# A second wait in front of each quad of indirect gathers on GpSimd

## What is computed

```python
def _gnn_layer(edge_index, x, edge_attr, norm, We, be, Wn, bn):
    src, dst = (edge_index[0], edge_index[1])
    parts = [x[src], x[dst]]
    if edge_attr is not None:
        parts.append(edge_attr)
    e = jax.nn.relu(jnp.concatenate(parts, axis=-1) @ We + be)
    msg = e * norm[:, None] if norm is not None else e
    agg = jax.ops.segment_sum(msg, dst, num_segments=x.shape[0])
    x_new = jax.nn.relu(jnp.concatenate([x, agg], axis=-1) @ Wn + bn)
    return (x_new, e)
```

## Time and profile before

| what | us |
|---|---|
| median of three runs | 2675.99 |
| lowest and highest of them | 2674.0, 2693.58 |
| the profiled execution | 2685.29 |
| its span, first to last instruction | 2683.2 |
| TensorE busy | 2142.4 (80%) |
| VectorE busy | 1447.8 (54%) |
| GpSimd busy | 1001.1 (37%), of it 824.7 in the 864 gathers of L1512 |
| mean share of TensorE's full clock | 0.875 |

### The profile page before, as it was taken

One profiled execution on the slowest core, in us unless ns is written; L12 is line 12 of the kernel. 1 busy time (PEld: TensorE's weight loads), 2 busy tenths in 40 slices (PEclk: granted clock), 3 DMA queues, 4 the chain that ended last, 5 costly groups with the idle time before them and its releaser, 6 DMA issues. The chain is left out here.

```text
span 2683.2 us, 48362 instructions
## 1 busy us (share of the span) xinstructions
PE 2142.4 (80%) x14264; PEld 1585.6 (59%) x14264; DVE 1447.8 (54%) x4661; ACT 653.0 (24%) x1271; POOL 1001.1 (37%) x1015
## 2 busy tenths in 40 slices
PE   7666679999999657777777678888888677888885
PEld 4222234444444347666666578787877577777774
DVE  6988832332332446656666455555555455555555
ACT  0246731221221122222222322222222211111111
POOL 0765400000000035555555245454553454555550
PEclk8777789999999768878888899999999888889887
DMA  2123550000000343333333255555553333433431
GB/s 81 25 57 83 95 47 1 0 0 0 0 0 0 120 127 107 116 102 114 105 112 108 83 164 160 154 164 165 162 162 117 103 101 97 112 105 106 112 106 38
DMA packets 193650, 242.15 MB, mean 90 GB/s; under 512 B 56276, under 2 KB 120047, under 8 KB 192799
## 3 DMA queue, kind: packets, MB, share of 16 engines
q1 hardware_dynamic: 161023, 172.73, 22.3%
q0 software_dynamic: 31840, 57.21, 9.1%
q10 hardware_dynamic: 576, 9.44, 0.9%
HBM read 149.75 MB, written 69.88 MB: 82 GB/s over the span
## 5 line engine op out<-in xcount | busy, mean ns | idle before, releaser
L1512 POOL DMA_INDIRECT rows<-p_dram,src_i x864 | 824.7, 954 | 751.9 <-PE psum L1623 441.8
L1744 DVE TENSOR_TENSOR agg_t<-psum,agg_t 128x128 f32 x1380 | 394.1, 286 | 466.6 <-remote 263.6
L1603 PE MATMUL psum<-w_c,before 128*128 128x128 f32 x1840 | 440.8, 321 | 24.2 <-issue 23.8
L1592 PE MATMUL psum<-p_sb,pair_src 128*128 x1032 | 257.7, 330 | 151.3 <-issue 85.6
L1677 ACT ACTIVATE rows<-rows 128x512 f32<-128x512 f32 x216 | 136.1, 630 | 901.1 <-DVE rows L1737 608.3
L893 PE MATMUL psum<-adj,parts 128*128 (+2 forms) x1750 | 339.7, 351 | 5.8 <-ACT agg L972 4.4
L1603 PEld LDWEIGHTS psum<-w_c,before 128*128 128x128 f32 x1840 | 305.3, 207 | 27.4 <-issue 27.3
L1728 DVE TENSOR_SCALAR hot_w<-col_f,dst_loc,weight 128x128 f32<-128x128 f32 x864 | 308.5, 360 | 0.5
L1623 PE MATMUL psum<-hot_w,rows 128*128 128x128 f32 x1728 | 279.8, 307 | 29.4 <-issue 27.6
L1592 PEld LDWEIGHTS psum<-p_sb,pair_src 128*128 128x128 f32 x1032 | 188.2, 224 | 175.7 <-issue 173.6
L1599 PE MATMUL psum<-q_parts,hot_all 128*128 x2592 | 270.2, 229 | 15.5 <-issue 15.4
(11 more groups left out here) (241 smaller groups left out, 2590.4 us busy)
## 6 DMA issues: line engine op xcount, KB each, us to landing
e_dram<-after SPq DMA_DIRECT2D x230, 256.0 KB
before<-e_dram SPq DMA_DIRECT2D x230, 256.0 KB
adj<-stage SPq DMA_DIRECT2D x196, 97.8 KB
pair_rows<-sorted_rows SPq DMA_DIRECT2D x129, 128.0 KB
rows<-p_dram,src_i POOLq DMA_INDIRECT x864
hot_all<-dst_rows ACTq DMA_DIRECT2D x2, 3072.0 KB, 15.0
p_dram<-p_sb SPq DMA_DIRECT2D x6, 384.0 KB
records<-record_of,place_i POOLq DMA_INDIRECT x128
```

What stands on the lines that cost most here:

```text
L1512: nc.gpsimd.indirect_dma_start(out=rows[:, b % ROWS, m * D:(m + 1) * D], out_offset=None, in_=p_dram, in_offset=bass.IndirectOffsetOnAxis( ...
L1592: nc.tensor.matmul(o, pair_src[:, i % PAIRS, m, :], t["p_sb"][:, bass.ds(values[m], 1), :], start=True, stop=False)
L1603: mm = nc.tensor.matmul(o, before[:, q % BEFORE, m * P:(m + 1) * P], w_c[:], start=False, stop=True)
L1744: nc.vector.tensor_tensor(a, psum[:, A_BANKS[q % len(A_BANKS)], m * P:(m + 1) * P], a, ALU.add).then_inc(agg_on, 1)
```

## The change

Ahead of the first gather of quad b, from b = 4 on, GpSimd also waits until all four gathers of quad b - 1 have landed. `landed(b)` is the count that `rows_in[b % 4]` has then; it is the same count that `add` waits for on VectorE.

```diff
         def _(pool):
+            def landed(b):
+                earlier = nth * len(range(b % ROWS, REST_QUADS, ROWS))
+                return 16 * QUAD * (earlier + b // ROWS + 1)
+
             def further_rows():
...
                 if b >= ROWS:
+                    pool.wait_ge(rows_in[(b - 1) % ROWS], landed(b - 1))
                     pool.wait_ge(summed, slot_of(b - ROWS) + 1)
```

## The result

The change costs about half a per cent where it was first timed: 2690.37 us median (19 runs, 2675.16 to 2699.26) against 2674.31 us (19 runs) for the kernel before, ratio 1.0048 with the interval 1.0026 to 1.0069. A second comparison gave 2678.40 against 2674.52 us, ratio 1.0028 (1.0004 to 1.0052). Predicted were 2679 us, within 2668 to 2712. The figure fits, but its reason does not: the profile after shows rival B's mechanism in all three passes. The time hardly moved because one pass gained what the two others lost, so the figure is right by luck.

A forecast was written before the change was run, and what follows sets the result against it. TensorE, the busiest engine, was taken to pace the passes and GpSimd's gathers; the added wait would mostly hide in the adds' margin. The median 2676 plus 3 us gave 2679 us, range 2668 to 2712.

The forecast's parts named there:

- rival B: Landing paces the kernel: 0.47 us more a quad in passes one and two, 20 + 27 us, time 2723; chance 0.21.
- slack that hides the wait: Gathers before the adds: rows lie finished 7.7 to 10.2 us, so the wait costs 0 to +15 us; chance 0.74.
- The start behind the landing: GpSimd's next first gather after the last packet: 0.3 us semaphore plus 0.26 us start, together 0.6 us.
- The landing: Time from a quad's last gather to its last packet: about 1.6, 2.0 and 1.3 us in passes one, two, three.
- a small stretch: Landings lengthen on meeting SP's transfers at another time; half of 0.5 us a quad gives 15 to 20 us.
- level with what they needed: GpSimd's idle time a quad in passes one and two: 2.2 and 2.6 us there, 2.2 and 2.6 needed.
- The releasers: What ends waits: landing for well over half of 204 first gathers in passes one and two; TensorE still for VectorE's adds.
- the prediction's own test: Profile after: adds released by the landing of rows would mean the landing paces the kernel.
- Pass three has room: GpSimd's gathers in pass three: 2.5 us idle a quad there, 1.9 needed, so the added wait costs 0 us.
- the replay: Recurrence over all 216 quads by the trace's times: passes one, two, three end 1, 2, 0 us later; +3 taken.
- C: Later gathers put fewer packets beside SP's loads, for which TensorE waits: up to 25 us faster, 2651; chance 0.05.
- GpSimd does not pace anybody: GpSimd in the passes: busy half the time, idle 240 to 259 us a pass before gathers, paced by TensorE's sums.

The follow-up runs named there:

- first pair of profiles: Kernel before and changed kernel, each profiled in the first timing: 2674.31 against 2690.37 us median, ratio 1.0048.
- second pair of profiles: Both kernels, unchanged, profiled once more in a later comparison: before 2674.52 us, changed 2678.40 us, ratio 1.0028.
- the last experiment: Kernel before with the wait for the landing added in pass three alone, timed once more: 2366.14 us against 2228.94, ratio 1.0621.
- The run with quarter transfers: Changed kernel with SP's loads of the layer before and its stores cut to a quarter of their columns: 2577.61 us, ratio 1.1551 to the kernel before.

## Why the prediction was right, and where it was wrong

2679 us lies within 0.5% of what was measured, and that is luck. The mechanism that was given the most weight, slack that hides the wait, did not hold in any pass. The landing paced the gathers, as in B, and passes one and two together lost 20 to 42 us, within what B says; pass three gained as much by something that was in no rival.

**The start behind the landing: right.** 0.3 us for the semaphore and 0.26 us for the start were taken, 0.6 in sum. In the profile after, the median from a quad's last packet to the next first gather is 0.62, 0.65 and 0.60 us. The 0.73 us of rival B belongs to a wait in the sequencer, and exchanging the waits showed it (1.08 us).

**The landing: the term that was mis-sized.** 1.6, 2.0 and 1.3 us were taken, and that is what before has (1.68, 2.07, 1.32). After the change they are 1.91, 2.46 and 1.50 us: 0.2 to 0.5 us more than was taken (0.1 to 0.3 us more than before in the second pair of profiles), where the margin that decided was put at 0.2 us a quad. The text named this way to fail ("if it stretches when its time moves") and gave it 0.21 together with a price of 15 to 20 us for a small stretch. The weights stood the wrong way round. The reading that two of the three passes were level with what they needed was itself the warning: a term of 1.3 to 2.6 us, held fixed, decided it by 0.2.

The rule of the Trainium skill that was weighed ("DMA: Bandwidth & Descriptors", section "Anatomy of one DMA") gave 2.15 us always, by estimate 7.1 us a quad. The medians from one quad's first gather to the next one's are 7.15, 7.45 and 6.61 us in the profile after, so as a price of a gather chain it was near the truth for two passes. The trace agrees with its size and not with "always": landings range from 1.2 us to 5.6 us.

**The releasers: wrong.** First gathers released by the landing in well over half of the cases was right (197 of 204, the number for all three passes), an idle sum "nearly the same" was right by accident (261.1, 302.1, 225.0 for 240, 259, 253 us), and "adds still released by TensorE" was wrong. By the prediction's own test this is B.

**Pass one and two: B's direction, and its size.** B's price for a small stretch was 15 to 20 us, for 0.47 us a quad 20 + 27. Measured: +10.5 and +31.6 us in the first pair of profiles, -5.0 and +25.4 in the second, and +34 us by the experiment with the wait in these two passes alone.

**Pass three: the step that failed.** "Pass three has room", cost 0, held for the sum that stood behind it (1.50 + 0.6 = 2.1 us needed a quad, 2.5 there), and yet 42 of its 72 adds were late. What was wrong is what stands under it, in the replay and in the first paragraph: TensorE's times were carried over as a property of the work. They hold 368 us of pauses that the profile puts down to nothing, and 282 us of those vanish with the added wait. As TensorE got faster, its adds caught up with the landings. So pass three gained 29 to 45 us (the two pairs of profiles, and the experiment with the wait there alone), which no rival had. C (faster, 0.05) had another mechanism, a shorter wait for SP's loads: this wait fell from 12.8 to 6.2 us in pass three, a sixth of the gain.

**"GpSimd does not pace anybody": true of the chips with pauses.** The idle 2.2 to 2.6 us a quad on GpSimd was slack lent by TensorE's pauses. Where these are absent a quad of before takes 5.3 us in pass one (381 us by 72), 5.0 of them GpSimd's own four gathers (4.69 + 0.30), and the chain of landings needs 7.0 (the median of pass three in the last experiment). The run with quarter transfers, the nearest there is to the changed kernel on such a chip, is 349 us over the kernel before. An estimate for the whole change: its passes of the other chip, 1605 us, less 381 + 416 + 382 gives 426 us, a ratio of 1.19. The changed kernel itself was not run on such a chip.

**What stays open.** What the pauses are. The same program has them in three comparisons and hardly any in three others, and where it has them, they are in a stage without these gathers too. What takes them away is open as well: late adds that hold TensorE up, or gathers of two quads no longer in flight together. The first fits a TensorE that runs ahead of the supply of its instructions, but no run showed that supply. Against the second as the whole cause: in pass one of the last experiment all 68 first gathers start ahead of the landing of the quad before, and the short pauses are 26 us. The runs without gathers, which would have shown whether the gathers have a part in the pauses, fell on chips without them. Whether it is the chip or something else that differed between comparisons isn't settled either.

## What to carry to other kernels

A wait for the landing of one's own last transfer turns a queue into a chain: four gathers, landing, start, here 4.7 + 1.5 to 2.5 + 0.6 us a quad. Compare that sum with the consumer's beat at its best, not with the beat of one trace, and where the two are within a few tenths of a microsecond, treat the case as open. Slack that consists of waits "for nothing that the profile shows" isn't slack to spend. And a change that reads as neutral on one chip should be timed on more: here 0.3 to 0.5% in two comparisons stood beside 15% for a lighter form of the same kernel in a third.

## What the hardware did that was not expected

- The same program took 2674 to 2677 us in some comparisons and 2227 to 2229 us in others, each within some 1%; the longer time has 368 us of short pauses of TensorE in the passes, in steps of 0.7 and 1.4 us, and more time at the lower clock.
- Of two waits ahead of an indirect DMA on GpSimd, the one written first rides on the instruction (0.61 us from the last packet to the start), the other is the sequencer's (1.08 us). The order of two lines was worth some 65 to 72 us.
- The landing of a quad's last 64 KB gather, 1.2 us after its end at the shortest, took up to 5.6 us, and 4.1 us beside 0.73 MB of SP's transfers that were issued while the quad was being gathered.
